# Gated attention kernel: the order of the projection products in a software pipeline, shifted by half a step, with K ahead of Q

## The reference

```python
# attention, 16 heads of 16 channels, per batch of 128 tokens
Qh = (q @ Wq + bq); Kh = (k @ Wk + bk); Vh = (v @ Wv + bv)      # q = layernorm(x), k = v = ctx
scores = Qh Kh^T / sqrt(10);  masked keys get -1e9
out = softmax(scores) @ Vh
x = x + tanh(g_xattn) * out
# expert layer on layernorm(x): 8 experts, each takes its 1024 best tokens
scores = (x_flat @ Wg.T).T; top_vals, token_idx = top_k(scores, n // 8)
y = (silu(xg @ W1^T) * (xg @ W3^T)) @ W2^T * softmax(top_vals)
x = x + tanh(g_ffn) * scatter_add(y)
```

## Time and profile before

| | us |
|---|---|
| three runs | 958.1, 955.09, 960.22; median 958.1 |
| the profiled execution | 957.71, span 956.0 |
| TensorE busy | 776.2 (81%) |
| VectorE busy | 595.6 (62%) |
| ScalarE busy | 540.5 (57%) |
| GpSimd busy | 398.9 (42%) |
| first scores of the attention | 43.85 after the start |
| length of one group of four batches in the loop | 33.2 to 33.7, twice 36.3 |

### The profile page before, as it was taken

The page is one execution under the profiler, slowest core; times in us unless marked ns, Lnnn a source line. Parts: engine busy times, 40 slices in busy tenths (PEclk is TensorE's granted clock), DMA queues, the critical chain, the costliest instruction groups (busy, mean ns, idle before and its releaser), DMA issues. The chain is left out here.

```text
span 956.0 us, 22544 instructions
## 1 busy us (share of the span) xinstructions
PE 776.2 (81%) x7256; PEld 610.2 (64%) x7256; DVE 595.6 (62%) x1481; ACT 540.5 (57%) x1065; POOL 398.9 (42%) x791
## 2 busy tenths in 40 slices
PE   3479888977988898898898874118999999999994
PEld 1346666665666576566566663116888888888984
DVE  1357677766776776777586674885564664654540
ACT  2245576666576656656557574645555555555641
POOL 3442354334335424433433311214547447457425
PEclk9689999999999989999899997558999999999998
DMA  4955586677659558666854711503436436434224
GB/s 121 242 129 153 167 210 160 182 205 177 174 169 239 141 159 231 148 179 189 202 148 112 187 62 68 177 14 126 113 77 122 111 65 132 111 68 62 49 25 45
DMA packets 98899, 130.38 MB, mean 136 GB/s; under 512 B 13648, under 2 KB 61936, under 8 KB 98800
## 3 DMA queue, kind: packets, MB, share of 16 engines
q1 hardware_dynamic: 86544, 112.48, 43.5%
q0 software_dynamic: 12288, 17.05, 10.8%
HBM read 52.10 MB, written 25.71 MB: 81 GB/s over the span
## 5 line engine op out<-in xcount | busy, mean ns | idle before, releaser
L737 DVE TENSOR_REDUCE m_sb<-a_ps 128x4 f32<-128x512 f32 x256 | 165.3, 676 | 23.2 <-PE a_ps L956 22.5
L590 ACT ACTIVATE p_t<-b_ps 128x512 f32<-128x512 f32 x256 | 147.6, 587 | 56.5 <-PE b_ps L969 54.8
L1281 POOL DMA_INDIRECT out<-y,idx_add x64 | 100.4, 1568 | 110.7 <-ACT y L1340 100.0
L956 PE MATMUL a_ps<-k_st,q_st 97*128 97x128 bf16 x1024 | 100.9, 222 | 27.3 <-DMA k_st<-k_part 18.4
L489 POOL TENSOR_TENSOR q_part<-q_rest,q_part 128x512 bf16<-128x512 f32 x32 | 37.0, 1157 | 184.1 <-ACT q_part L561 184.1
L956 PEld LDWEIGHTS a_ps<-k_st,q_st 97*128 97x128 bf16 x1024 | 74.5, 99 | 61.3 <-issue 51.0
L969 PE MATMUL b_ps<-q_st,k_st 99*128 99x128 bf16 x1024 | 100.6, 221 | 4.7 <-ACT p_t L590 4.7
L1650 PE MATMUL bank<-x_hi,w_hi 128*128 128x512 f32 x256 | 101.7, 397 | 1.5 <-DVE x_lo L1497 1.5
L1650 PE MATMUL bank<-x_lo,w_hi 128*128 128x512 f32 x256 | 100.3, 392 | 0.0
L1650 PE MATMUL bank<-x_hi,w_lo 128*128 128x512 f32 x256 | 100.1, 391 | 0.0
L1518 DVE TENSOR_TENSOR act_h<-act_h,bank 128x512 f32<-128x512 f32 x64 | 44.0, 688 | 85.4 <-PE bank L1650 82.8
(11 more groups left out here) (207 smaller groups left out, 1700.2 us busy)
## 6 DMA issues: line engine op xcount, KB each, us to landing
q_st<-q_part SPq DMA_DIRECT2D x96, 256.0 KB, 4.9
k_st<-k_part SPq DMA_DIRECT2D x96, 256.0 KB, 4.2
w<-in_w_t SPq DMA_DIRECT2D x24, 512.0 KB, 5.0
rows_scratch<-xg SPq DMA_DIRECT2D x16, 528.0 KB, 4.5
x_in<-in_x SPq DMA_DIRECT2D x16, 512.0 KB, 5.0
c_t<-in_ctx_t SPq DMA_DIRECT2D x16, 512.0 KB, 5.2
x_res<-in_x SPq DMA_DIRECT2D x16, 512.0 KB, 4.1
out<-x SPq DMA_DIRECT2D x16, 512.0 KB, 3.0
```

The source lines that it names most:

```text
L590: act.activation(p_t[b.s % 2][:, 4 * q:4 * q + 4, :], b_ps[q % 2][:].rearrange("p (h s) -> p h s", s=P), ACT.Exp, scale=SCALE).then_inc(ex ...
L737: dve.tensor_reduce(m_sb[b.s % 2][:, 4 * q:4 * q + 4], a_ps[q % 2][:].rearrange("p (h s) -> p h s", s=P), AX_X, ALU.max).then_inc(max_done, 1)
L956: mm = pe.matmul(a_ps[q % 2][:, i * P:(i + 1) * P], q_st[g.p][0:A_K, h, tok], k_st[g.p][0:A_K, h, tok], start=True, stop=True)
L1281: pool.indirect_dma_start(out[:, :], bass.IndirectOffsetOnAxis(ap=idx_add[e % 2][:, st:st + 1], axis=0), y[st][:], None, compute_op=ALU.ad ...
```

## The change

The front order becomes rows, K, V after Q: u = 0, 1 are the transposes, u = 2, 3 give K, u = 4, 5 give Q, u = 6, 7 give V. The positions move by half a step: step j issues products 2j+1 and 2j+2 of group g+1, and quarter 2 of step 3 issues product 0 of group g+2 already. The instructions that take the products out, split and stack them move with them: both stacks are issued by SP in step 2 (K ahead of `max_rows`, Q behind it), and the last of `mid_k` stands at the end of step 1 on ScalarE. On GpSimd `ln1` now stands between the K splits of m = 0 and those of m = 1. The number of instructions, their sizes and their buffers are the same. The constants are loaded in the order x, ctx, K weights, mask, Q weights.

```diff
@@ SP, step
                 if b.j == 2:
                     place_scores(g.on(-3))
-                    stack_q(g.on(1))
+                    stack_k(g.on(1))
                 if b.j == 3:
                     store_rows(g.on(-3))
-                    stack_k(g.on(1))
                 max_rows(b.back(1))
+                if b.j == 2:
+                    stack_q(g.on(1))
@@ GpSimd, step
                 for m in range(KD):
                     if b.j == 1:
-                        split_q(g.on(1), m)
-                    if b.j == 2:
                         rest_k(g.on(1), m)
                         split_k(g.on(1), m)
+                        if m == 0:
+                            ln1(g.on(2))
+                    if b.j == 2:
+                        split_q(g.on(1), m)
                 if b.j == 0:
                     ln2_scales(g.on(-2))
-                if b.j == 1:
-                    ln1(g.on(2))
@@ ScalarE, step
                 exp(b.back(3), 3)
                 if b.j == 0:
-                    xn_t_out(f, 0)
+                    if first(g):
+                        xn_t_out(f, 0)
+                    xn_t_out(f, 1)
                 if b.j == 1:
-                    hi_q(f, 0)
+                    mid_k(f, 0)
                 if b.j == 2:
-                    hi_k(f, 0)
+                    hi_q(f, 1)
                 neg_hi(b.back(1))
...
                 if b.j == 2:
+                    mid_q(f, 0)
                     normalise2(g.on(-2), (0, 1))
...
                 exp(b.back(2), 0)
                 exp(b.back(2), 1)
                 if b.j == 1:
-                    mid_q(f, 0)
+                    hi_k(f, 1)
+                    hi_q(f, 0)
                 if b.j == 2:
-                    mid_k(f, 0)
-                if b.j == 0:
-                    xn_t_out(f, 1)
-                if b.j == 1:
-                    hi_q(f, 1)
-                if b.j == 2:
-                    hi_k(f, 1)
-                if b.j == 2:
+                    mid_q(f, 1)
                     normalise2(g.on(-2), (2, 3))
                 if b.j == 3:
                     normalise(g.on(2), (2, 3))
+                if b.j == 3:
+                    xn_t_out(g.on(2), 0)
                 exp(b.back(2), 2)
                 pv_copy(b.back(3))
                 if b.j == 0:
                     router_out(g.on(-3))
+                    hi_k(f, 0)
                 if b.j == 1:
-                    mid_q(f, 1)
-                if b.j == 2:
                     mid_k(f, 1)
@@ VectorE, step
                 if b.j == 1:
                     stats(b.group.on(2), range(GB))
-                if b.j == 1:
-                    rest_q(f, 0)
+                    make_k(f, 1)
                 if b.j == 2:
-                    make_k(f, 0)
+                    rest_q(f, 1)
                 if b.j == 3:
-                    make_v(f, 0)
+                    make_v(f, 1)
                 neg_mid(b.back(1))
                 maximum(b, 1)
                 maximum(b, 2)
                 finish(b.back(4))
-                if b.j == 1:
-                    rest_q(f, 1)
-                if b.j == 2:
-                    make_k(f, 1)
-                if b.j == 3:
-                    make_v(f, 1)
-                maximum(b, 3)
+                if b.j == 0:
+                    make_k(f, 0)
+                if b.j == 1:
+                    rest_q(f, 0)
+                if b.j == 2:
+                    make_v(f, 0)
+                maximum(b, 3)
@@ TensorE, step
                     if q in (0, 2):
-                        front(g.on(1), 2 * b.j + q // 2)
+                        u = 2 * b.j + q // 2 + 1
+                        if u == 1 and first(g):
+                            front(g.on(1), 0)
+                        front(*((g.on(1), u) if u < 8 else (g.on(2), 0)))
```

More of the change, by code:

```diff
@@ L266, in steps, with first @@
                 step(eng, Batch(g // 2, 4 * (g % 2) + j, NB))
+    def first(g):
+        return isinstance(g.k, int) and 2 * g.k + g.p == 0
     def at_last(b, g, j):
@@ L395, in _ @@
             load_x(Group(0, 0, NG))
+            load_c(Group(0, 0, NG))
+            load_const(wk_sb[:], square(wk), s_wk)
+            load_const(bk_sb[:], bk, s_wk)
+            load_const(mask_nat[:], mask, s_misc)
             load_const(wq_sb[:], square(wq), s_wq)
             load_const(bq_sb[:], bq, s_wq)
[L398 to L401, removed]
             load_const(wv_sb[:], square(wv), s_wv)
@@ L413, in _ @@
             sp.wait_ge(s_bias_st, 16)
-            stack_q(Group(0, 0, NG))
+            stack_k(Group(0, 0, NG))
             for u in range(GB):
@@ L418, in _ @@
             load_c(Group(0, 1, NG))
-            stack_k(Group(0, 0, NG))
+            stack_q(Group(0, 0, NG))
             def step(sp, b):
@@ L516, in _ @@
             for m in range(KD):
-                split_q(g, m)
-            for m in range(KD):
                 rest_k(g, m)
                 split_k(g, m)
+            for m in range(KD):
+                split_q(g, m)
             ln1(Group(0, 1, NG))
@@ L551, in hi_q @@
                 if g.ok:
-                    f_wait(g, 2 + m)
+                    f_wait(g, 4 + m)
                     if m == 0:
@@ L559, in mid_q @@
                 if g.ok:
-                    act.wait_ge(f_free[m], g.times(4, 2))
+                    act.wait_ge(f_free[m], g.times(4, 3))
                     act.activation(q_part[:, MID, m, :], q_rest[:, m, :], ACT.Copy).then_inc(q_mid, 1)
@@ L564, in hi_k @@
                 if g.ok:
-                    act.wait_ge(f_free[m], g.times(4, 3))
+                    act.wait_ge(f_free[m], g.times(4, 2))
                     if m == 0:
@@ L626, in router_out @@
                     act.activation(scores_of(g), m_ps[:, R_AT:R_AT + P], ACT.Copy).then_inc(r_out, 1)
-            act.wait_ge(s_wq, 32)
             g = Group(0, 0, NG)
@@ L633, in _ @@
             for m in range(KD):
+                hi_k(g, m)
+                mid_k(g, m)
+            act.wait_ge(s_wq, 32)
+            for m in range(KD):
                 hi_q(g, m)
                 mid_q(g, m)
-            for m in range(KD):
-                hi_k(g, m)
-                mid_k(g, m)
             normalise(Group(0, 1, NG), range(GB))
@@ L714, in make_k @@
                 if g.ok:
-                    dve.wait_ge(f_done, g.times(8, 5 + m))
+                    dve.wait_ge(f_done, g.times(8, 3 + m))
                     dve.wait_ge(s_c[g.p], g.turn(32, 32))
@@ L846, in _ @@
             dve.tensor_scalar(bias_nat[:], mask_nat[:], -1.0, MASKED, ALU.add, ALU.mult).then_inc(s_bias, 1)
+            dve.wait_ge(s_wk, 32)
+            for m in range(KD):
+                make_k(g, m)
             dve.wait_ge(s_wq, 32)
@@ L849, in _ @@
                 rest_q(g, m)
-            dve.wait_ge(s_wk, 32)
             dve.wait_ge(s_wv, 32)
-            for m in range(KD):
-                make_k(g, m)
             for i in range(2):
@@ L925, in front @@
                 elif u < 6:
-                    wt, src = (wq_sb, xn_t) if u < 4 else (wk_sb, c_t[g.p])
+                    wt, src = (wk_sb, c_t[g.p]) if u < 4 else (wq_sb, xn_t)
                     if isinstance(g.k, int):
-                        pe.wait_ge(*((s_wq, 32) if u < 4 else (s_wk, 32)))
+                        pe.wait_ge(*((s_wk, 32) if u < 4 else (s_wq, 32)))
                     if u < 4:
+                        pe.wait_ge(s_c[g.p], g.turn(32, 32))
+                    else:
                         pe.wait_ge(f_free[0], g.times(4, 1))
                         pe.wait_ge(f_free[1], g.times(4, 1))
-                    else:
-                        pe.wait_ge(s_c[g.p], g.turn(32, 32))
                     for k in range(KD):
```

## The result

Twenty runs of each: 959.62 us (956.92 to 963.12) against 956.49 (954.69 to 961.39), a ratio of 1.0028 [1.0018, 1.0039]. The kernel became 0.3% slower, which lies inside the 0.5% that the prediction counted as no change; "slower", to which I had given the largest chance (0.42), did not come. The profiled execution took 960.6 us, span 958.8, against 957.7 and 956.0: 2.9 us more where I had forecast 4.4. The direction held, and the total is near only because errors inside the sum cancelled, which is luck. The table is my own tally from the timelines of TensorE; a group is counted from the first transpose of row maxima in its step 0 to the next.

A forecast was written before the change was run, and what follows sets the result against it. TensorE was taken as the bound, with holes of 6.1 us in a 33.4 us group. The terms +7 + 0.7 + 1 - 2.8 - 0.7 - 0.8 gave +4.4 us on 957.7: 962 us, range 944 to 975 for 8 in 10.

The forecast's parts named there:

- `ln1`'s block: GpSimd's `ln1` still delays a half of K, so ScalarE waits 3.9 us at `mid_k(1)`, as long as before.
- 2.0 at `scores_t_`: Step 2: TensorE waits for an exponential that stands behind `mid_k(1)` on ScalarE, a new hole of 2.0 us.
- second V product: It waits for `make_v(0)` on the late VectorE: 1.45 us, against 0.9 for K to V before.
- row product: Step 3: product 0 of group g+2 waits for the second pair of `normalise`, a new hole of 1.2 us.
- the block is covered: Rival: GpSimd early or ScalarE slack hides the block, about 938 us, half of it 950; in part or wholly, 22%.
- the stacks land late: Rival: twelve stack DMAs leave within one step, Q's last; at 7 us landing, 972 us; 20% shared with the clock.
- The granted clock: ... I leave this cost as it is.: Two long loop groups with half-clock stretches cost 2.8 us each; this cost was taken as unchanged.
- The rival: The clock falls more often: every second group, 8 us more, 970; 20% shared with late stacks.
- I take +0.7, ten groups: +7: Loop groups 4 to 13: each period 0.7 us longer, +7 us in all.
- Q's two halves: Hole while ScalarE, then VectorE take out Q's product: 1.0 us, against 0.9 before.
- group 14 ... 30 to 31: -2.8: Group 14 has no `ln1`, so no block and no row product in step 3: 30 to 31 us from 33.5, -2.8.
- Group 15 begins without the low clock that followed that hole: -0.7: Group 15 no longer starts with the low clock that followed the hole of 3.10 us behind group 14: -0.7 us.

The follow-up runs named there:

- e1: Changed kernel with `ln1` on GpSimd moved behind the K splits of both halves in step 1: 947.09 us, 0.9889 of the kernel before.
- e2: Kernel before with `ln1` on GpSimd moved ahead of the Q splits in step 1: 931.86 us, 0.9749 of the kernel before.
- e10: Changed kernel with two Newton steps in place of three in `ln1`, its place kept: 941.64 us against 961.46, ratio 0.9791.
- e9: Changed kernel with `ln1` behind the K splits and Q's two splits set between its links: 946.74 us, ratio 0.9856.
- e11: Changed kernel with `ln1` behind the K splits and step 3's second `normalise` pair ahead of `exp(b-2,1)`: 948.05 us against 955.52, ratio 0.9917.
- e13: Changed kernel with `stack_q` back in step 3, behind `store_rows` and ahead of `max_rows`: 974.26 us against 955.52, ratio 1.02.

## Why the prediction was right in the path and wrong in the sum

**Right.** That the change moves `ln1`'s block instead of removing it, with 3.9 us of waiting forecast and 3.75 found, and that it costs TensorE 2.0 at `scores_t_` in step 2; e1, e2 and e10 show the block as a cause and not only as a neighbour. The chain of waits behind it also came as forecast (second V product 1.4 for 1.45, row product 1.1 for 1.2). The start, group 0 and groups 1 to 3 came within 0.3, but other executions of the changed kernel differ by more than that there. The rivals "the block is covered" and "the stacks land late" don't hold in the loop; the second becomes the bound as soon as the block goes (e1, e9, e11), or one more copy stands ahead of Q's (e13), for the margin was as small as I had it: 0.3 to 1.0 us for 1.

**Wrong, first: "The granted clock: ... I leave this cost as it is."** The rival had it more often at 2.8 each. The long groups had cost 2.4 each to begin with: 36.3 was the length of a window and not of the group, 35.9. The clock did fall in seven of ten groups in place of two, but each stretch is half as long and costs 0.3: it begins at the end of the hole at `scores_t_`, and the work that it holds back runs into the hole before the second V product, which goes. Placement and lost hole are read from the trace of seven groups; no run moves a stretch by itself. In the experiment with the filled hole a short stretch could take up only the 0.74 at the head of the group, and it cost some 0.8 (34.35 against 33.6), which speaks for it. The clock's cost went from 4.7 to 2, which I had at no change: 2.9 of the loop's missing 6.2.

**Second, the period.** "I take +0.7, ten groups: +7": 0.37 was measured between undisturbed groups. I had stepped to 34.1 and found 33.93; and I set it against the mean of 33.5 while the true mean of the eight was 33.56. The sum of holes gave +0.8, measured 6.6 against 6.1 gives +0.5 for this one pair of groups (33.90 against 33.41): the holes that I priced too high are Q's two halves (1.0, measured 0.8), the row product (1.2, 1.1) and the second V product (1.45, 1.4). The term was a difference of two sums of seven holes, each good to 0.1 or 0.2. That is 3.3 of the 6.2.

**Third, groups 14 and 15**, with the other sign: "group 14 ... 30 to 31: -2.8" and "Group 15 begins without the low clock that followed that hole: -0.7". Measured -1.0 and +1.1. I used the loop's claim that Q's last DMA leaves 6 us before the next group where the holes that made those 6 us were just what I took out of group 14: there it leaves 2.8 before, and lands 5.8 after its issue has ended. The late landing of a stack set the head of group 15 in both orders. The 0.7 for the low clock behind it rested on no row of its own, and a longer low stretch came in its place.

The errors, -6.2 and +3.6, with 0.3 in the small terms and 0.7 behind the attention, which no part of the change touches and which I can't account for, turn 4.4 into 2.8. That is this one pair of executions: with the other traces of the changed kernel the loop's error is near -5, so the two large errors are real and their near balance is chance.

## What to carry to other kernels

A serial chain of tiny instructions on a helper engine costs where it stands in its queue, so moving work past it changes who pays, and here one line that moves the chain itself was worth 2.5% where reordering the front cost 0.3%. When a step removes a hole, take the window that transfers had from the shortened schedule, group by group: the landing that was hidden by the hole is the next bound. And price a stretch at the lower clock by the work that it holds back less the hole that it runs into: their number is not their price.

## What the runs showed of the hardware

In the loop the stretches at 1.2 GHz lasted 3.4 or 6.8 us in every trace. In the kernel before, where they fell changed from one execution to the next (333.3 and 469.9, then 298.6 and 435.1) while their number and the length of the loop stayed (340.3 and 340.4). The six DMAs of one stack took 4.41 us (Q) and 6.11 us (K) to issue in one group of the changed kernel: behind the first three of K, SP waited for the parts of the second half. GpSimd's links cost 0.38 us each in the loop for a busy time of 0.2, and 0.29 where it is written out (4.65 us for 16), without the second count: about half of the block is hand-over between dependent instructions, not work.
